# Decoder layer in float32 on one Trainium2 core: transposes of attention weights and normalized rows made by row halves in banks of their own

## Time and profile before

| | |
|---|---|
| time, median of 3 runs (lowest to highest) | 624.79 us (624.72 to 625.19) |
| the profiled execution's own time | 625.01 us |
| its span, first to last instruction | 623.2 us |
| busy: TensorE, weight loads | 615.1 us (99%), 544.1 us (87%) |
| busy: VectorE, ScalarE, GpSimd | 506.6 (81%), 428.6 (69%), 349.3 us (56%) |
| instructions | 19898 |

### The profile page before, as it was taken

The page is one execution under the profiler, slowest core; times in us unless marked ns, Lnnn a source line. Parts: engine busy times, 40 slices in busy tenths (PEclk is TensorE's granted clock), DMA queues, the critical chain, the costliest instruction groups (busy, mean ns, idle before and its releaser), DMA issues.

```text
span 623.2 us, 19898 instructions
## 1 busy us (share of the span) xinstructions
PE 615.1 (99%) x7309; PEld 544.1 (87%) x7309; DVE 506.6 (81%) x980; ACT 428.6 (69%) x1489; POOL 349.3 (56%) x739
## 2 busy tenths in 40 slices
PE   8999999999999999999999999999999999999998
PEld 5789988888899888888999989999999888998987
DVE  6898899889988899977887788777777759888776
ACT  4788888888888888887565777675667653434443
POOL 4899376855777576854588767466466533010100
PEclk9999999999999999999999999999999999999999
DMA  7955000000000000032200000000000000010001
GB/s 199 390 224 205 1 3 3 2 2 2 1 2 2 1 3 1 19 137 69 49 11 19 3 3 19 2 3 2 2 2 3 2 1 2 2 35 5 29 34 35
DMA packets 10101, 23.78 MB, mean 38 GB/s; under 512 B 1650, under 2 KB 6050, under 8 KB 9122
## 3 DMA queue, kind: packets, MB, share of 16 engines
q1 hardware_dynamic: 7858, 14.77, 7.0%
q0 software_dynamic: 1440, 7.08, 3.3%
q10 hardware_dynamic: 720, 0.79, 0.4%
HBM read 20.53 MB, written 2.10 MB: 36 GB/s over the span
## 4 chain that ended last, share of the span: by engine, by line
PE 92%; DVE 3%; ACT 2%; issue 1%; DMA 0%; POOL 0%; SPq 0%; DVEq 0%; ACTq 0%; POOLq 0%
PE bank L576 14%; PE bank L578 14%; PE bank L577 14%; PE pair L648 10%; PE bank L691 9%; PE pair L576 7%; PE pair L577 7%; PE pair L578 6%; PE bank L824 5%; PE bank L636 2%; PE bank L594 2%; ACT e_sb L1065 1%; PE bank L969 1%; DVE ri L1329 1%; PE pair L969 1%
## 5 line engine op out<-in xcount | busy, mean ns | idle before, releaser
L453 POOL TENSOR_SCALAR p_f<-e_sb,rsum 128x128 f32<-128x128 f32 x256 | 93.5, 386 | 39.0 <-DVE rsum L1562 38.4
L361 POOL TENSOR_SCALAR p_int<-e_sb,rsc 128x128 int16<-128x128 f32 x256 | 103.3, 424 | 6.3 <-issue 5.9
L1156 ACT ACTIVATE e_sb<-bank,neg_max 128x128 f32<-128x128 f32 x256 | 90.8, 379 | 0.1
L648 PE MATMUL pair<-aT_sb,v_sb 64*64 64x128 f32 x1920 | 77.0, 275 | 0.0
L1065 ACT ACTIVATE e_sb<-si 128x128 f32<-128x128 int16 x256 | 75.4, 303 | 0.8 <-DVE si L1351 0.8
L1508 DVE TENSOR_REDUCE neg_max<-bank 128x4 f32<-128x512 f32 x64 | 41.2, 685 | 34.6 <-PE bank L691 34.3
L691 PE MATMUL bank<-k_sb,q_sb 64*64 64x128 f32 x2048 | 67.7, 270 | 0.7 <-DVE k_sb L1334 0.6
L648 PEld LDWEIGHTS pair<-aT_sb,v_sb 64*64 64x64 f32 x1920 | 54.4, 132 | 8.3 <-issue 1.3
L691 PEld LDWEIGHTS bank<-k_sb,q_sb 64*64 64x64 f32 x2048 | 58.4, 133 | 2.3 <-DVE k_sb L1334 1.4
L1207 ACT COPY o_raw<-pair 128x512 f32<-128x512 f32 x29 | 17.0, 585 | 60.5 <-PE pair L648 60.5
L1449 DVE SCALAR_TENSOR_TENSOR si<-s_sgn,bank 128x512 int16<-128x512 bf16 x64 | 43.2, 680 | 18.6 <-ACT s_sgn L1110 18.5
(11 more groups left out here) (193 smaller groups left out, 2123.8 us busy)
## 6 DMA issues: line engine op xcount, KB each, us to landing
wB_raw<-in_wB SPq DMA_DIRECT2D x1, 3072.0 KB, 13.8
wB_hi<-in_wB POOLq DMA_DIRECT2D x1, 3072.0 KB, 11.5
wqk_raw<-in_wqk SPq DMA_DIRECT2D x8, 256.0 KB, 7.9
x_sb<-in_x SPq DMA_DIRECT2D x3, 512.0 KB, 18.3
out<-x_sb SPq DMA_DIRECT2D x6, 256.0 KB, 2.3
wqk_hi<-in_wqk POOLq DMA_DIRECT2D x5, 256.0 KB, 7.1
wp_raw<-in_wp SPq DMA_DIRECT2D x1, 1024.0 KB, 12.5
wp_hi<-in_wp POOLq DMA_DIRECT2D x1, 1024.0 KB, 8.3
```

What stands on the lines that cost most here:

```text
L361: i = nc.gpsimd.tensor_scalar(p_int[:, half, t, :], e_sb[:, half, t, :], rsc[:, half, t:t + 1], -0.5, ALU.mult, ALU.add)
L453: i = nc.gpsimd.tensor_scalar(p_f[:, half, t, :], e_sb[:, half, t, :], rsum[:, half, t:t + 1], 0.0, ALU.mult, ALU.add)
L648: last = pe.matmul(o_pair[hh * DH:(hh + 1) * DH, side, b * P:(b + 1) * P], v_sb[at, 2 * side + b, h0:h0 + DH], aT_sb[at, GB * hh + 2 * sid ...
L1156: last = nc.scalar.activation(e_sb[:, (s - 1) % 2, t, :], s_ps[hh][:, (t % 4) * P:(t % 4 + 1) * P], ACT.Exp, bias=neg_max[:, t:t + 1], sca ...
```

## The change

- The eight weight transposes of a B slot become 16: for each of eight tiles, rows 0 to 63 go to the first bank and rows 64 to 127 to the second, 64 columns each. Both banks must be free before the first. `aT_sb` is copied by bank, which is now by row half.
- Normalized rows likewise: 16 transposes of 64 rows a set, one semaphore step after all; high and low part by bank. The first block of A waits for both low parts.
- B's values: a slot makes one batch with 512 columns (three matmuls) in place of two batches with 256, so value columns of four head pairs are complete after four slots.
- `o_raw` is copied in two pieces of 256 columns, bank 7 first (`b_raw7`), then bank 6 (`b_raw`). Queries wait for the first, keys for the second.
- At the start: moments, inverse deviations and normalized rows in two halves, VectorE's first weight subtraction between the halves, 13 filler matmuls in place of 20.
- In A: `y_out` half 0 stands behind the reciprocal, half 1 at the end of slot 3; in slot 7 the third sign stands before the fourth exponential; in slots 1 and 2 a sign goes ahead of four exponentials.
- GpSimd casts the first context only after the keys of A's last slot; `b_add_bias` in B's first three slots waits for a low part of A's output.
- TensorE's loop over C's middle groups is written out.

Left out below: new semaphores, renumbered counts of `ln_T`, the second place of each repeated edit, `a_exp`'s new range argument.

```diff
--- before.py
+++ after.py
...
@@ -201,6 +201,7 @@
     g_veps, ln_x0, w1_hi = sem("g_veps"), sem("ln_x0"), sem("w1_hi")
+    ln_b0, ln_m0, g_v0, g_r0 = sem("ln_b0"), sem("ln_m0"), sem("g_v0"), sem("g_r0")
     c_rh, c_gh, c_hh, c_lh = sem("c_rh"), sem("c_gh"), sem("c_hh"), sem("c_lh")
@@ -239,6 +240,13 @@
         return isinstance(g, int) and g == 0 and s < LAG
+    def half_rows(t, rows):
+        return t[:, :, :].rearrange("p k (b r q) -> p r (k b) q", r=2, q=DH)[:, rows, :, :]
+    def as_blocks(bank):
+        return bank[:, :].rearrange("p (a q) -> p a q", q=DH)
@@ -340,6 +348,19 @@
                                     base=0, pattern=[[-1, P]], channel_multiplier=1).then_inc(g_const, 1)
+            def first_inv_std():
+                for j in range(2):
+                    at = slice(2 * j, 2 * j + 2)
+                    pool.wait_ge((ln_m0, ln_mv)[j], 1)
+                    nc.gpsimd.tensor_scalar(veps[:, at], mv[:, at, 1], EPS, (FIX * GROW) ** -2.0, ALU.add,
+                                            ALU.mult).then_inc(g_v0, 1)
+                    pool.wait_ge(g_v0, j + 1)
+                    nc.gpsimd.tensor_tensor(rstd[:, at], veps[:, at], mhalf[:, at], ALU.pow).then_inc(g_r0, 1)
+                pool.wait_ge(g_r0, 2)
+                nc.gpsimd.sem_inc(g_veps, 1)
+                nc.gpsimd.sem_inc(g_rstd, 1)
             def inv_std(n, scaled=False):
@@ -404,6 +425,7 @@
                     pool.wait_ge(ld_ctx, 16)
+                    wait(pool, a_fx, BLOCKS * G - 1)
                     nc.gpsimd.tensor_copy(cT_hi[:, :], cT_raw[:, :]).then_inc(b_chi, 1)
...
@@ -491,7 +513,10 @@
                     b_weights(NP * g + s - 1, (s - 1) % 2)
-                wait(pool, b_olo, NP * g + s - LAG + 1)
+                if first and s < LAG:
+                    pool.wait_ge(a_olo, NP * G + s - LAG + 1)
+                else:
+                    wait(pool, b_olo, NP * g + s - LAG + 1)
                 if first and s == 3:
@@ -582,24 +607,32 @@
-            keep_busy(20)
+            keep_busy(13)
             pe.wait_ge(g_const, 4)
+            def normed_rows(b):
+                for kt in range(KD):
+                    for rows in range(2):
+                        at = slice(rows * DH, (rows + 1) * DH)
+                        to = (kt * GB + b) * DH
+                        last = pe.transpose(proj_ps[rows][:, to:to + DH], xn[at, b, kt * P:(kt + 1) * P], ident[at, at])
+                return last
...
                     prev_reads(kt)
-                    for b in range(GB):
-                        last = pe.transpose(proj_ps[kt][:, b * P:(b + 1) * P], xn[:, b, kt * P:(kt + 1) * P],
-                                            ident[:, :])
-                    last.then_inc(ln_T, 1)
+                for b in range(GB):
+                    last = normed_rows(b)
+                last.then_inc(ln_T, 1)
...
                 if kind == 0 and s == 0:
-                    wait(pe, ln_lo, 2 * g + 1)
+                    wait(pe, ln_lo, 2 * g + 2)
                 elif kind < 2 or n < LAG:
...
@@ -769,7 +798,7 @@
                     else:
-                        wait(pe, b_raw, n - LAG)
+                        wait(pe, b_raw7, n - LAG)
                         if n == LAG:
@@ -781,6 +810,8 @@
                         pe.wait_ge(b_k, LAG)
+                    else:
+                        wait(pe, b_raw, n - LAG)
                     if s == 0:
@@ -792,12 +823,9 @@
                         wait(pe, b_clo, g + 1)
-                    col = QW * (s // 2)
-                    for i in range(2):
-                        b = 2 * (s % 2) + i
-                        last = split3(out_[:, i * QW:(i + 1) * QW], [t[:, b * P:(b + 1) * P] for t in (cT_hi, cT_lo)],
-                                      [w[:, col:col + QW] for w in (wvB_hi, wvB_lo)], i == 0, True,
-                                      skip_group_check=True)
+                    b, col = s % GB, TOK * (s // GB)
+                    last = split3(out_[:, :], [t[:, b * P:(b + 1) * P] for t in (cT_hi, cT_lo)],
+                                  [w[:, col:col + TOK] for w in (wvB_hi, wvB_lo)], True, True)
                 last.then_inc(b_blk, 1)
@@ -809,7 +837,6 @@
                 for hh in range(2):
-                    out_ = (drain_pT_ps if drain else pT_ps)[hh]
                     if s == 0:
@@ -820,8 +847,12 @@
                             pe.wait_ge(m_sum, s - 3)
-                    for b in range(GB):
-                        last = pe.transpose(out_[:, b * P:(b + 1) * P], p_f[:, half, GB * hh + b, :], ident[:, :])
+                for t in range(8):
+                    for rows in range(2):
+                        at = slice(rows * DH, (rows + 1) * DH)
+                        out_ = (drain_pT_ps if drain else pT_ps)[rows]
+                        last = pe.transpose(out_[:, t * DH:(t + 1) * DH], p_f[at, half, t, :], ident[at, at])
                 last.then_inc(b_T, 1)
...
@@ -927,7 +958,7 @@
                 gg = g if s >= LAG else g - 1
-                v_count = NP * gg + 2 * (p // 2) + 2
+                v_count = NP * gg + GB * (p // GB) + GB
                 b_attend_quarters(n - LAG, p, v_count, 0)
@@ -1020,7 +1051,7 @@
                 c_slot(0, s, first=True)
-            with pe.Fori(1, G - 1) as g:
+            for g in range(1, G - 1):
                 for s in range(NF):
@@ -1040,9 +1071,9 @@
             def xnT_high(n):
-                for kt in range(KD):
-                    wait(act, ln_T, 2 * n + kt + 1)
-                    nc.scalar.copy(xnT_hi[:, kt, :], proj_ps[kt][:, :]).then_inc(ln_hi, 1)
+                wait(act, ln_T, n + 1)
+                for rows in range(2):
+                    nc.scalar.copy(half_rows(xnT_hi, rows), as_blocks(proj_ps[rows])).then_inc(ln_hi, 1)
...
@@ -1090,17 +1122,22 @@
                     sign_of(g, 3 * s + 2)
+                early = 3 if s == NP - 1 else 4
                 if not (first and s == 0):
-                    a_exp(n - 1, (s - 1) % 2, 0)
+                    a_exp(n - 1, (s - 1) % 2, 0, range(early))
                 if not (first and s <= LAG):
                     sign_of(g, 3 * s + 2)
+                if s == NP - 1:
+                    a_exp(n - 1, (s - 1) % 2, 0, range(early, 4))
                 if first and s == 0:
                     high_part(2)
+                if first and 0 < s < LAG:
+                    sign_of(g, 3 * s + 3)
                 if not (first and s == 0):
...
                     xnT_high(g + 1)
-                if first and s < LAG:
+                if first and s == 0:
                     sign_of(g, 3 * s + 3)
@@ -1204,8 +1241,11 @@
                         wait(act, b_olo, n - LAG)
-                        nc.scalar.copy(o_raw[:, :].rearrange("p (a f) -> p a f", a=2), o_pair).then_inc(b_raw, 1)
+                        for side in (1, 0):
+                            at = slice(side * 2 * P, (side + 1) * 2 * P)
+                            nc.scalar.copy(o_raw[:, at], o_pair[:, side, :]).then_inc((b_raw, b_raw7)[side], 1)
                         wait(act, b_pj, n - LAG)
+                        wait(act, b_raw7, n - LAG + 1)
                         wait(act, b_raw, n - LAG + 1)
...
@@ -1290,15 +1332,18 @@
-            def norm_moments():
-                for b in range(GB):
+            def norm_moments(batches=range(GB)):
+                for b in batches:
                     i = V.bn_aggr(mv[:, b, :], bn_st[:, b, :])
-                i.then_inc(ln_mv, 1)
+                i.then_inc(ln_mv if GB - 1 in batches else ln_m0, 1)
...
                 wait(dve, T_count[0], T_count[1])
-                wait(dve, g_rstd, n + 1)
+                if isinstance(n, int) and n == 0:
+                    wait(dve, g_r0, 2 if GB - 1 in batches else 1)
+                else:
+                    wait(dve, g_rstd, n + 1)
                 for b in batches:
@@ -1310,17 +1355,21 @@
                 norm_stats(0, 0, (b,))
+                if b == 2:
+                    dve.wait_ge(ln_b0, 1)
+                    norm_moments((0, 1))
             dve.wait_ge(ln_bn, 1)
-            norm_moments()
-            norm_apply(0, 0, (ln_T, 0))
+            norm_moments((2, 3))
+            norm_apply(0, 0, (ln_T, 0), (0, 1))
             dve.wait_ge(w0_hi, 1)
...
             V.tensor_tensor(lo, raw, hi.bitcast(F32), ALU.subtract).then_inc(w0_lo, 1)
+            norm_apply(0, 0, (ln_T, 0), (2, 3))
...
             def xnT_low(n):
-                for kt in range(KD):
-                    wait(dve, ln_hi, 2 * n + kt + 1)
-                    V.tensor_tensor(xnT_lo[:, kt, :], proj_ps[kt][:, :], xnT_hi[:, kt, :].bitcast(F32),
+                for rows in range(2):
+                    wait(dve, ln_hi, 2 * n + rows + 1)
+                    V.tensor_tensor(half_rows(xnT_lo, rows), as_blocks(proj_ps[rows]), half_rows(xnT_hi, rows).bitcast(F32),
                                     ALU.subtract).then_inc(ln_lo, 1)
...
@@ -1432,12 +1481,10 @@
```

(13 more changed lines are left out.)

35 lines of the change are left out of this document (17 added, 18 removed).

## The result

The changed kernel takes **616.57 us** (median of 4 runs, 616.41 to 616.67) where the kernel before took 624.84 beside it (4 runs, 624.72 to 625.19): ratio 0.9866, 95% interval 0.9849 to 0.9884, 8.27 us less. The profiled execution took 616.61 us, its span went from 623.2 to 615.0.

What follows compares the result with a forecast made beforehand. TensorE was taken to bound the kernel, with 92% of the chain that ended last. Terms summing to -10.0 us took the profiled 625.01 to 615.0, with the median 0.2 lower at 614.8 us; range 610.5 to 621.5.

Steps and rivals of the forecast that it cites:

- main term: Weight transposes of cross-attention slots: row halves work at once, net 0.256 us saved a slot, -7.9 us over 31 slots.
- Pair pace: Cross-attention weight transposes: a pair of half transposes takes 0.057 us, bounds 0.055 to 0.12.
- the first rival: Weight transposes: each pair's 128-column load binds at 0.109 to 0.12 us, +5 to +8.8 us in all; chance 0.13.
- Queries ahead of the output copy: Cross-attention slots: queries need only the first 256-column copy, of bank 7; counted at nothing, cover 0.08 us.
- The values: Cross-attention value projection: three 512-column matmuls a slot for six of 256 columns, -0.7 us in all.
- Group ends of the cross-attention: Four normalized-row sets there: TensorE waits about 0.2 us, leaving under 0.1 of gain each, -0.3 us together.
- Drain: First drain slot: both transpose halves need the attention output's copy, which comes as two copies ending later, +0.3 us.
- Start: First block needs both subtractions, against an earlier first half of the statistics: +0.5 us, bounds -0.5 and +2.
- `y_out`: Bias output, three places: moving it behind the reciprocal and the slot's rest takes most of a 0.23 us wait, -0.6.
- Fourth group end of the self-attention: Normalized-row set there: GpSimd's context cast waits for the keys and a block is signed earlier, -0.5 us.
- GpSimd bias: Bias addition at 278.92 waits for VectorE's 1.57 us subtraction, for which TensorE is idle 0.50 us: -0.5 us.
- Feed-forward: Three normalized-row sets there: 0.416 us saved less two array crossings, -0.1 us each, -0.3 together.

Runs made afterwards that it cites:

- experiment 12: The changed kernel with weight transposes loading 96 of the 128 columns of a half (output differs); 617.12 us in one run.
- experiment 1: The kernel before with only the 16 weight transposes by row halves, copied by bank, and one 512-column output copy; 624.93 us, ratio 0.9995.
- experiment 4: The changed kernel with full weight transposes again and nothing else undone; 621.43 us, ratio 0.9937.
- experiment 5: The changed kernel with the projected output copied by one 512-column copy again; 621.77 us, ratio 0.9943.
- experiment 7: The changed kernel with the old value projection, six 256-column matmuls instead of three of 512; 617.82 us, ratio 0.9881.
- experiment 10: Experiment 9's kernel, with VectorE subtracting the normalized rows' high part ahead of the context's at group ends; 615.93 us, ratio 0.9855.
- experiment 2: The changed kernel with full transposes of the normalized rows at all 12 sets, weights still in halves; 616.69 us, ratio 0.9866.
- experiment 9: The changed kernel with full normalized-row sets up to the third cross-attention group, halves after, output copies turned round in the last slot; 616.22 us.
- experiment 6: The changed kernel with the start of the kernel before; 617.42 us, ratio 0.9878.
- experiment 8: The changed kernel with `y_out` ahead of the reciprocal again and without GpSimd's two new waits; 619.60 us, ratio 0.991.
- experiment 11: The changed kernel without GpSimd's two new waits, VectorE's order staying as changed; 618.35 us, ratio 0.9891.
- experiment 3: The changed kernel with all eight weight transposes of rows 0 to 63 first, then all eight of rows 64 to 127; 626.45 us, ratio 1.002.

## Why the prediction was right, and where not

The side and the range hold: 616.57 for 614.8, in 610.5 to 621.5. The gain is 8.3 us for a forecast 10.0. The mechanism of the main term holds on TensorE (transposes in different row halves run at once), but it pays only with the split output copy, which the prediction priced at nothing. Term by term:

- **Pair pace**: 0.057 forecast, 0.063 measured, set by the load (experiment 12), with 0.05 more for the first pair. The bound of 0.12 was far off, and the first rival needed 0.089. The Trainium skill's rule in "TensorE: Matmul & The Clock Gate", section "LDWEIGHTS (loading the stationary operand)", by which (an estimate from its figure) a pair could not be under 107 ns, does not hold for these float32 transposes: 63 ns here.
- **The step that failed** is "Queries ahead of the output copy", "counted at nothing, cover 0.08". The sum compared the end of the copy's record (0.54 after the first transpose) with TensorE's readiness (0.62), and left out the 0.145 from that end to the matmul it releases. With it the copy is last (0.51 + 0.145 = 0.65 measured). The same omission is in the reading of the kernel before: of the 0.18 "for the crossing back", 0.02 was a wait for the copy. Experiments 1, 4 and 5 show what hung on it: the split copy, priced at nothing, carries 4.8 us, since without it the halves gain nothing. In the changed kernel the wait costs only 0.01 a slot, because TensorE itself is ready at 0.64, forecast 0.62.
- **The main term** was over-sized: 0.256 forecast a slot, 0.21 measured (0.866 to 0.653, where the sum had 0.872 to 0.616), so -6.6 for 31 slots, not -7.9. The values gave 0.03 a slot, -1.0 for -0.7, and experiment 7 takes back 0.86 (0.04 a slot).
- **Group ends of the cross-attention**: the forecast was a wait of 0.2 that leaves under 0.1 of gain each. The slot after the end is longer than its neighbours by 0.66, 0.40 and 0.38 us (7.57, 7.31 and 7.29 for 6.91), and the set saves 0.24: a loss of 0.4, 0.15 and 0.15, against 0.24 gained at the fourth. Together +0.5 for -0.3. Two causes: the sum ran the wait against the value matmuls' old order, in which four transposes needed the first subtraction only; and at the first end VectorE's subtraction of the context (1.2 us beside GpSimd) delays it (experiment 10).
- **Drain** +0.3: from the last slot's scores to the feed-forward's first matmul 2.67 us before, 2.99 now. Right.
- **Start** +0.5: 10.42 to 10.88. About right, though the same start scatters by 0.65 us between profiles. The halves lose 0.7 (experiments 2, 9, 10); what the new start itself gives stays open (experiment 6).
- **`y_out`** -0.6: the three slots that end at 109.8, 176.0 and 242.2 gained 0.3 each, -1.0 in all. Experiment 8 takes back two of them. Under-sized.
- **Fourth group end of the self-attention** -0.5 and **GpSimd bias** -0.5: between the two traces 0.5 is gained in the slot at the self-attention's end and 0.4 at the opening. About right. Experiment 11 puts 0.35 and 0.4 of them down to GpSimd's waits.
- **Feed-forward** -0.3: the three sets gain 0.13 together between the two traces, and experiment 2 gives back 0.12. Over-sized. The two later drain slots, 0.2 each, belong to the main term.

Measured terms: -6.6 - 1.0 + 0.5 + 0.3 + 0.5 - 1.0 - 0.5 - 0.4 - 0.1 = -8.3, the whole of what is seen. So the 1.7 us that are missing from the forecast are the main term's 1.3, the group ends' 0.8 and small change, less the 0.7 that `y_out` and the values gave more.

## What to carry over

A wait that ends together with the work above it has no row of its own. Before pricing a shorter stretch, add the release (here 0.145 us from the end of the copy's record to the matmul) to every other input of what comes next; here shorter transposes were worth 0.00 alone, an earlier copy 0.02, and both together 0.21 us a slot. A set written to both banks at once frees neither early: do it where nothing waits for the first bank, and fill bank after bank where something does. Where an idle engine's side work stretches a subtraction on the path, as here from 0.69 to 1.57 us, it is worth a wait. And one profile of each kernel does not settle what a start is worth: the same code began its first block anywhere within 0.65 us.

## What was unexpected of the hardware

- Float32 transposes that load 64 rows by 128 columns and move 64 follow each other every 0.063 us within a row half, and both halves keep that pace at once, each with a bank of its own. With rows in turn (experiment 3) the second half's chain starts 0.31 us after the first half's, before the first is through.
- VectorE's 512-column subtraction takes 0.69 us alone and 1.57 beside GpSimd's addition, on operands of the same size and type; GpSimd's two waits bought 0.75 us where it can be seen in the trace.
- In otherwise equal slots the twelve 512-column matmuls take 2.83 us in the changed kernel and experiments 2, 5, 6 and 10, 2.85 in experiment 4, and 2.86 to 2.87 in experiments 3, 8, 9 and 11, at a granted clock of 1.0 or 0.999: up to 0.03 or 0.04 a slot, 0.9 us or more in all. No edit among these touches them. This was not settled; it is the size of the differences between the best versions.
- The same pair of engines explains the long slot of experiments 6, 8, 9 and 10, 0.44 to 0.49 us in the second cross-attention group, the one that merges rows. VectorE and TensorE there in the changed kernel, then in experiment 6:

```profile
366.46 1.65 DVE L1348 TENSOR_SCALAR xn<-x_sb,mv,rstd 128x256 f32<-128x256 f32 x2
...
370.90 0.39 PE L601 MATMUL bank<-wB_hi,cT_lo 128*128 128x512 f32 x1
...
366.75 2.71 DVE L1345 TENSOR_SCALAR xn<-x_sb,mv,rstd 128x256 f32<-128x256 f32 x2
...
371.31 0.50 PE L601 MATMUL bank<-wB_hi,cT_lo 128*128 128x512 f32 x1
```

In these four profiles the first of VectorE's two normalizations lasts 2.3 us beside four GpSimd operations and ends 0.2 us after the last of them; in the changed kernel it lasts 0.9 beside the same four. VectorE's copies of the transposed weights then end 1.05 us later, and TensorE's value block and merge matmul wait for them. Counted from the transposes, both engines start that work at the same time to 0.02 us in the changed kernel and in experiment 6, so what decides between 0.9 and 2.3 isn't shown.
- Not tried: in the changed kernel the query block's bank 7 is written last by the attention. Ordering those matmuls ahead of bank 6's would start the copy earlier, but TensorE is ready only 0.01 us before the copy, so alone it would gain next to nothing; with shorter transposes, as in experiment 12, 0.07 a slot would come free (0.653 less 0.58; an estimate).
